# A Mamba scan kernel: more products with B on GpSimd, and its rows of B one column further

## The reference, cut to what matters

```
def step(h, inp):
    d_l, b_l, c_l, x_l = inp
    h = exp(d_l[:, :, None] * A) * h + (d_l * x_l)[:, :, None] * b_l[:, None, :]
    y_l = einsum('ben,bn->be', h, c_l)
    return (h, y_l)
```

## Time and profile before

| what | value |
| --- | --- |
| median of 3 runs | 1806.34 us (1803.77 to 1809.05) |
| the profiled execution's own time | 1808.85 us |
| its span in the trace | 1807.1 us |
| TensorE busy | 1696.5 us, 94% |
| VectorE busy | 1475.4 us, 82% |
| ScalarE busy | 1071.7 us, 59% |
| GpSimd busy | 1055.5 us, 58% |

### The profile page before, as it was taken

The page is one execution under the profiler, slowest core; times in us unless marked ns, Lnnn a source line. Parts: engine busy times, 40 slices in busy tenths (PEclk is TensorE's granted clock), DMA queues, the critical chain, the costliest instruction groups (busy, mean ns, idle before and its releaser), DMA issues. The chain is left out here.

```text
span 1807.1 us, 26494 instructions
## 1 busy us (share of the span) xinstructions
PE 1696.5 (94%) x9313; PEld 1339.5 (74%) x9313; DVE 1475.4 (82%) x2320; ACT 1071.7 (59%) x1872; POOL 1055.5 (58%) x649
## 2 busy tenths in 40 slices
PE   8898989899999989867999999999999999999999
PEld 3555666666666666655788888888899788888888
DVE  6899999999999999999897677776356886666664
ACT  7887877878787786787544344443444444444442
POOL 3899999999899998999832222220545322222220
PEclk9999999999999999978999999999999999999999
DMA  6333333333333333353011111121000021111111
GB/s 215 101 94 106 107 94 110 106 107 95 111 95 114 97 106 100 104 175 113 1 36 31 35 31 35 36 59 30 1 0 1 1 55 43 46 46 43 46 49 41
DMA packets 113806, 127.20 MB, mean 70 GB/s; under 512 B 18704, under 2 KB 64912, under 8 KB 113552
## 3 DMA queue, kind: packets, MB, share of 16 engines
q1 hardware_dynamic: 113680, 125.60, 24.2%
HBM read 97.24 MB, written 4.72 MB: 56 GB/s over the span
## 5 line engine op out<-in xcount | busy, mean ns | idle before, releaser
L395 POOL TENSOR_TENSOR m_U<-m_U,m_C 128x1024 f32<-128x1024 f32 x255 | 554.8, 2189 | 74.5 <-DVE m_U L966 74.2
L542 PEld LDWEIGHTS m_y<-ident,m_U 128*128 128x128 f32 x2048 | 250.5, 147 | 104.3 <-issue 73.9
L966 DVE TENSOR_TENSOR_SCAN m_U<-m_dA,m_carry,m_U 128x512 f32<-128x512 f32 x256 | 311.4, 1266 | 5.2 <-ACT m_dA L795 4.3
L966 DVE TENSOR_TENSOR_SCAN m_U<-m_dA,m_U 128x512 f32<-128x512 f32 x256 | 296.1, 1206 | 11.0 <-ACT m_dA L795 9.8
L542 PE MATMUL m_y<-ident,m_U 128*128 128x128 f32 x2048 | 281.9, 284 | 18.9 <-POOL m_U L395 18.6
L795 ACT ACTIVATE m_dA<-high,m_negA 128x512 f32<-128x512 f32 x256 | 172.1, 685 | 65.9 <-DVE m_U L966 65.9
L795 ACT ACTIVATE m_dA<-even,m_negA 128x512 f32<-128x512 f32 x256 | 170.5, 684 | 54.4 <-DVE m_U L966 52.4
L1265 POOL TENSOR_TENSOR SW<-g_Rt 128x512 f32<-128x512 f32 x32 | 40.0, 1281 | 255.0 <-DMA g_CT<-SW 235.3
L1265 POOL TENSOR_TENSOR SW<-f_Rt 128x512 f32<-128x512 f32 x32 | 41.0, 1310 | 210.5 <-DMA f_CT<-SW 210.5
L523 PE MATMUL m_psB<-m_stack,m_pick 128*128 128x512 f32 x188 | 97.2, 517 | 54.3 <-DVE m_U L949 52.9
L949 DVE TENSOR_TENSOR m_U<-even,m_psB 128x1024 f32<-128x1024 f32 x95 | 113.7, 1197 | 0.6 <-PE m_psB L523 0.6
(11 more groups left out here) (412 smaller groups left out, 4424.6 us busy)
## 6 DMA issues: line engine op xcount, KB each, us to landing
m_C<-bc_rows SPq DMA_DIRECT2D x256, 256.0 KB, 3.2
m_B<-bc_rows SPq DMA_DIRECT2D x68, 256.0 KB, 3.5
f_CT<-SW SPq DMA_DIRECT2D x128, 64.0 KB, 2.1
g_CT<-SW SPq DMA_DIRECT2D x128, 64.0 KB, 2.1
even<-in_ffn_w SPq DMA_DIRECT2D x16, 256.0 KB, 5.7
g_z_raw<-g_turned_z SPq DMA_DIRECT2D x112, 32.0 KB, 1.9
out<-res SPq DMA_DIRECT2D x7, 512.0 KB, 2.8
res<-in_x SPq DMA_DIRECT2D x1, 3072.0 KB, 12.6
```

Of the source, the lines that this page charges most:

```text
L395: pool.tensor_tensor(weighted[:, at, :, :], state[:, at, :, :], C[:, M % C_RING, :].unsqueeze(1).to_broadcast([P, PE_E, CHUNK]), ALU.mult) ...
L542: last = nc.tensor.matmul(y[:, t, j * P:(j + 1) * P], weighted[:, M % U_RING, j, t * P:(t + 1) * P], ident[:, :], start=False, stop=n == N ...
L966: nc.vector.tensor_tensor_scan(u, dA[:, s % A_RING, :], u, carry[:, e, n:n + 1] if q else 0.0, ALU.mult, ALU.add).then_inc(scan_done, 1)
```

## The change

Two edits. The first gives new lists: 6, 4, 7 and 5 products of 16 on GpSimd in the four passes of two chunks, and 5 in the very first pass. The second makes each buffer of B 513 columns wide and lets the rows start at the second column.

```diff
-    ON_POOL, AHEAD = ((3, 7, 10, 14), (3, 7, 11, 14), (2, 5, 8, 11, 14), (3, 6, 10, 14)), 3
+    FIRST_POOL, AHEAD = (3, 7, 10, 12, 15), 3
+    ON_POOL = ((2, 4, 7, 9, 12, 14), (3, 7, 11, 14), (2, 4, 6, 9, 11, 13, 15), (2, 5, 8, 11, 14))
...
-        B = sb("B", [P, B_RING, CHUNK])
+        B = sb("B", [P, B_RING, CHUNK + 1])[:, :, 1:]
...
-        pool_units = [M for M in range(ALL_UNITS) if M % N in ON_POOL[M // N % (2 * PASSES)]]
+        pool_units = [M for M in range(ALL_UNITS) if M % N in (ON_POOL[M // N % (2 * PASSES)] if M >= N else FIRST_POOL)]
```

## The result

The changed kernel takes 1791.03 us in the median of 4 runs (1789.89 to 1792.6), the kernel before 1807.39 us in 4. The ratio is 0.9913, with a 95% interval from 0.9895 to 0.993: 16.4 us less. The profiled executions say the same: 1791.06 us against 1808.85, spans of 1789.3 and 1807.1 us.

What follows compares the result with a forecast made beforehand. VectorE was taken to bound the Mamba part, GpSimd close behind. Pairs of chunks gain 3.3, 3.1, 4.6 and 6.4, together 17.4 us: 1808.85 becomes 1791.5, and 1790 allowing for the runs' lower median; range 1783 to 1803 us.

Steps and rivals of the forecast that it cites:

- The bound, the lists and VectorE's load: Mamba part: VectorE bounds; 19 products leave it, 21.1 us in all, making a middle pair's load 199.2 us.
- The second buffer starts at 514, even again: that product stays at 2.36 us: GpSimd products with B: first buffer 2.0 us, second still 2.36 us, so the mean is 2.19 us.
- odd and even: GpSimd products: a half whose inputs start an odd distance apart costs 1.76 ns a column, an even distance 2.12 ns.
- GpSimd becomes the bound: Middle pairs of chunks: GpSimd's load rises from 194.2 to 202.0 us, with VectorE (199.2) just under it.
- the rival in which all products are fast: All products with B last 2.0 us, GpSimd's load is 198.3 us, VectorE bounds everywhere: 1785.5 us; chance 0.08.
- The mutual waiting: Middle pairs: VectorE and GpSimd, nearly tied, wait for each other 1.5 us a pair, giving 203.5 us.
- that stretch: Everything after the Mamba part: counted as unchanged; the forecast is wrong if it moves by more than 1 us.
- The column changes nothing: Rival: all 87 products with B keep 2.32 us of cadence; only -7 us, so 1799.5; chance 0.22.
- The engines hold each other up: Rival: GpSimd lags at ends of passes; at 1.5 us in each of 16 passes +7 us, 1813; chance 0.08.
- The loads of B: SP queue: 19 more loads at odd byte addresses stay hidden, landing in 3.5 us, at most 8.2, within 10.5 us.

Runs made afterwards that it cites:

- the column alone: Kernel before with only the rows of B moved one column further, old lists kept; 1804.04 us, ratio 0.9986.
- 22 to 24: Products with B a pair on GpSimd raised from 22 to 24, both kernels being the changed one with rows of C moved too; 1790.14 us, then 1781.87 us.
- the lists alone: Kernel before with only the new lists, rows of B still at column 0; 1805.59 us, ratio 0.9992.
- the third column: Changed kernel with both buffers of B starting three columns further instead of one; one run, 1806.8 us.
- the sweep: Changed kernel with row starts of B varied over 0 to 15 columns, C over 0 to 7, state 1, 2 or 4; one run, 1801.33 us.
- 26 were badly placed: Changed kernel with rows of C moved and 26 products with B a pair on GpSimd, 6, 6, 7 and 7 by pass; 1792.43 us, ratio 0.9914.

## Why the prediction was right, and which step was not

**The bound, the lists and VectorE's load** were right. It forecast 199.2 us a middle pair and 198.9 were measured, and each product that left VectorE took its 1.11 us of work along (21.2 us for 19, above). What it is worth in time was less: 0.7 us a product from the column alone to the changed kernel, 0.8 from 22 to 24. The forecast let the whole of it reach the end wherever VectorE bounds and left VectorE's other waits as they were; its waits for decays grew from 13.0 to 19.8 us when the 19 products left.

**"The second buffer starts at 514, even again: that product stays at 2.36 us"** is the step that failed. I had read odd and even out of the product with C, from the observation that any place within four columns gave the same duration. The durations are indeed equal, but because each product has one half of either class: 513 columns pair a cheap distance with a dear one in every buffer. The mean of the new product was thus priced 2.19 us and is 2.00. My figure for a cheap product, 2.0 us, was right; what I missed is that a distance of 2 is cheap also. The product with C gives only the sum of two classes; that the two are odd and even was one way among several to split it, and I took it for the only one.

**"GpSimd becomes the bound"** fell with it: 197.3 us of work and not 202.0 (198.3 stood in the rival in which all products are fast). The condition of that rival held: all products with B are fast and VectorE bounds. Its time did not, 1785.5 against 1791.0. The Mamba part lost the 21 us that it gives, but the 2 us of VectorE's waits that it adds did not come, and the stretch after took 2.8 us more.

**The mutual waiting** of 1.5 us a pair was too much. In the kernel with the lists alone, where GpSimd is full, the middle pairs are 0.6 us longer than its work.

**Why the total is still right.** The Mamba part came out 3.6 us better than forecast (21.0 after 17.4 us), and the stretch after it, which I had counted as unchanged, 2.8 us worse, of which the lower granted clock can stand for 1.7 by estimate. I had said I would be wrong if that stretch moved by more than 1 us; it did, and no edit touches it. The spans add up as 1807.1 - 21.0 + 2.8 + 0.4 (the first scan was that much later) = 1789.3 us. So 1790 against 1791 is in part luck: two errors of opposite sign. The 21.0 itself is in part luck too. It is a difference of two single executions, and that of before had a long Mamba part; from the kernel with the column alone the same 19 products brought 14 us.

**The rivals.** "The column changes nothing" had the next best chance, 0.22, and is false: 2.00 after 2.36 us. "GPSIMD Engine Reference", section 3.1, of the Trainium skill explains the cost of the two-input product by its inputs taking turns at one read port. The page names no starting place; that the cost has nothing to do with it was my reading. The measured 2.00 and 2.37 us for the same shapes do not go against such turns, but one floor for every starting place does not account for them. "The engines hold each other up" did not come in the changed kernel; VectorE waited for GpSimd where all or half of the products with B were dear (13.7 us in all with the lists alone, 14.1 with the third column, 10.8 in the sweep) and where 26 were badly placed (9.6 us). None of these was slower than the kernel before. The loads of B at a moved column stayed hidden in the changed kernel: they landed in 3.5 us in the median and 8.8 at most (3.5 and 8.2 before), and GpSimd waited for none.

## What to carry to other kernels

Moving work between two engines takes its cadence off the one that bounds, until the other is full in any one stage: compare loads pass by pass, not in the sum, and let the stages with side work keep fewer. Less of it may reach the end: here 0.7 to 0.8 of 1.11 us, because waits for a third engine grew. Before moving work to a slower engine, look for what makes its instruction dear; here one column of padding was worth 15% of a product, and neither edit alone was worth more than 3 us. When equal durations seem to rule a variable out, check that no instruction is a sum of two halves that always fall in opposite classes.

## What the hardware showed that I had not expected

A GpSimd product of two fp32 inputs from SBUF, 128 x 1024, the second a row of 512 columns used twice, lasts 2.00 us if the second input starts 1 or 2 columns of 4 bytes after the first, counted within 16 bytes, and 2.37 us if 0 or 3. This rests on 342 products in one trace, with no overlap between the classes (1.987 to 2.054 and 2.344 to 2.400 us). The places are those of the program's columns; the trace shows no addresses. The place of the output made no difference. Why 1 and 2 differ from 3 is open. With the rows of C moved as well and 24 or 25 products a pair, the kernel takes 1781.9 and 1780.3 us: ratios of 0.9851 and 0.9847, where the change has 0.9913.
